# Turning a finished group's hidden state by a DMA of its 16-bit planes in place of TensorE's transposes

## What is computed

```python
h = jnp.maximum(_layernorm(x, axis=-1), 0.0)
x = x + _L3_gnn_ref(h, adj, nodemask, weight, w_ih, w_hh, b_ih, b_hh)

# _L3_gnn_ref, with A = (adj != 0)
for l in range(5):
    m = jnp.einsum('bnd,de->bne', h, weight[l])
    agg = jnp.einsum('bij,bid->bjd', A, m)
    h = _gru_cell(agg, h, w_ih, w_hh, b_ih, b_hh)   # r, z, n gates; h = (1-z)*n + z*h
return h * mask[..., None]
```

## Time and profile before

| | |
|---|---|
| device time, median of 3 runs | 686.35 us (685.84 to 688.16) |
| the profiled execution | 686.79 us, span from first to last instruction 684.7 us |
| granted PE clock, mean over the span | 0.995 |
| busy PE / DVE / ACT / POOL | 652.9 / 594.9 / 526.3 / 410.2 us |
| DMA queue q1, share of 16 engines | 23.9% |

### The profile page before, as it was taken

One profiled execution on the slowest core, in us unless ns is written; L12 is line 12 of the kernel. 1 busy time (PEld: TensorE's weight loads), 2 busy tenths in 40 slices (PEclk: granted clock), 3 DMA queues, 4 the chain that ended last, 5 costly groups with the idle time before them and its releaser, 6 DMA issues. The chain is left out here.

```text
span 684.7 us, 13204 instructions
## 1 busy us (share of the span) xinstructions
PE 652.9 (95%) x4380; PEld 424.8 (62%) x4380; DVE 594.9 (87%) x1349; ACT 526.3 (77%) x964; POOL 410.2 (60%) x367
## 2 busy tenths in 40 slices
PE   4899999999999999989999999999999999999995
PEld 3678888888888888865555444545555555555452
DVE  3877787777778877888999899999999999999995
ACT  3688888888888888867687787777877777877774
POOL 4556676677666666464774755555555555555554
PEclk9999999999999999999999999999999999999997
DMA  6111111111000110012232333333333343333532
GB/s 159 32 33 32 32 32 32 32 32 34 22 19 24 32 32 17 10 24 47 51 59 49 59 63 74 67 78 70 69 62 65 76 79 77 61 64 78 78 74 66
DMA packets 114691, 35.82 MB, mean 52 GB/s; under 512 B 87681, under 2 KB 114625, under 8 KB 114625
## 3 DMA queue, kind: packets, MB, share of 16 engines
q1 hardware_dynamic: 113424, 34.79, 23.9%
q10 hardware_dynamic: 1200, 0.20, 0.2%
HBM read 9.80 MB, written 4.19 MB: 20 GB/s over the span
## 5 line engine op out<-in xcount | busy, mean ns | idle before, releaser
L1553 POOL TENSOR_TENSOR h0T<-r,zh 128x512 f32<-128x512 f32 x80 | 104.1, 1302 | 140.4 <-DVE r L1587 140.2
L52 PE MATMUL psum<-t_parts,gru_w 128*128 128x512 f16 x720 | 181.7, 379 | 6.2 <-DVE t_parts L1577 6.2
L52 PE MATMUL psum<-h_parts,gru_w 128*128 128x512 f16 x720 | 181.8, 379 | 2.1 <-DVE r L1591 1.2
L52 PEld LDWEIGHTS psum<-h_parts,gru_w 128*128 128x128 f16 x720 | 69.7, 98 | 83.6 <-DVE r L1591 5.3
L52 PEld LDWEIGHTS psum<-t_parts,gru_w 128*128 128x128 f16 x720 | 65.4, 98 | 77.0 <-DVE t_parts L1577 15.5
L1547 POOL TENSOR_TENSOR zh<-z,h0T 128x512 f32<-128x512 f32 x80 | 102.7, 1284 | 15.0 <-ACT z L1525 14.7
L1522 ACT CAST t_parts<-psum 128x512 f16<-128x512 f32 x80 | 46.8, 585 | 60.9 <-PE psum L52 60.6
L1435 DVE CAST h_parts<-h0T 128x512 f16<-128x512 f32 x80 | 84.0, 1050 | 2.0 <-POOL h0T L1553 1.9
L691 POOL TENSOR_TENSOR prob<-prob,row_max 128x512 f32<-128x512 f32 x64 | 68.7, 1086 | 22.3 <-DVE row_max L1179 21.5
L1530 ACT ACTIVATE r<-r,gates_b 128x512 f32<-128x512 f32 x80 | 64.9, 812 | 17.5 <-DVE r L1581 17.2
L1525 ACT ACTIVATE z<-psum,gates_b 128x512 f32<-128x512 f32 x80 | 62.3, 778 | 5.8 <-PE psum L52 0.9
(11 more groups left out here) (135 smaller groups left out, 1199.4 us busy)
## 6 DMA issues: line engine op xcount, KB each, us to landing
x_all<-in_x SPq DMA_DIRECT2D x16, 256.0 KB, 3.3
adj<-in_adj SPq DMA_DIRECT2D x16, 256.0 KB, 2.9
out_x<-y SPq DMA_DIRECT2D x14, 256.0 KB, 2.3
h_nodes<-h_parts SPq DMA_TRANSPOSE x80, 3.0
out_x<-zT SPq DMA_DIRECT2D x2, 256.0 KB, 2.3
gw<-in_L_gnn_weight SPq DMA_DIRECT2D x1, 320.0 KB, 6.5
W<-in_L_gnn_W SPq DMA_DIRECT2D x2, 128.0 KB, 2.6
wi<-in_L_gnn_w_ih SPq DMA_DIRECT2D x1, 192.0 KB, 7.4
```

What stands on the lines that cost most here:

```text
L52: return nc.tensor.matmul(out, lhsT, rhs, start=start, stop=stop)
L1553: pool.tensor_tensor(state(now), by_graph(r[now.s][:, :]), by_graph(zh[now.s][:, :]), ALU.add)\
```

## The change

Twelve of the sixteen groups (those put out inside the rounds) are turned in another way; the last four stay as they were. The 32-bit numbers of a finished h are taken as two planes of 16-bit numbers. ACT copies each plane of the group into the buffer `halves` (`take_half`, two copies, in the slots e-5 and e-4, where e is the multiple of four at which the old slot list had begun the group's output and the old output came in slot e+1). SP issues one transposing DMA of all planes into `halves_nodes` in slot e-3 (`turn_halves`). ACT joins the planes into `last_h` (`put_half`, two copies, in slots e-2 and e+1). DVE makes the multiply-adds from `last_h`, two in slot e+2 and two in slot e+3, ahead of L1591 in place of after it, and SP stores in slot e+3. The new buffers are tiles of the first layers that are free by then.

```diff
+    halves, halves_nodes, last_h = first.y[3], first.adjT1[0], first.adjT
...
+    def halves_of(x):
+        return x.bitcast(U16).rearrange("p g (n t) -> p t g n", t=2)
+
+    def ended_before(j, back):
+        p, i = (j - back) // SLOTS, (j - back) % SLOTS // STREAMS
+        if (j - back) % STREAMS == 0 and 0 < p < ROUNDS and i > 0:
+            return Ended(p, i, 0)
...
-                    one_slot(p, i, s, Ended(p, i, 0) if p > 0 and i > 0 and s == 1 else None)
+                    one_slot(p, i, s)
...
+        def take_half(group, half):                                  # ScalarE
+            act.wait_ge(h_ready, group.h_count)
+            if group.count > 1:
+                act.wait_ge(halves_landed, 16 * (group.count - 1))
+            h = t["h0T"][:, bass.ds(group.first, GROUP), :]
+            a.copy(halves[:, 2 * half:2 * half + 2, :].bitcast(U16).rearrange("p u (v n) -> p (u v) n", v=2),
+                   halves_of(h)[:, half, :, :]).then_inc(halves_ready, 1)
+
+        def put_half(group, half):
+            act.wait_ge(halves_landed, 16 * group.count)
+            if group.count > 2:
+                act.wait_ge(out_ready, group.count - 2)
+            a.copy(halves_of(last_h[group.count % 2][:, :, :])[:, half, :, :],
+                   halves_nodes[:, 2 * half:2 * half + 2, :].bitcast(U16).rearrange("p u (v c) -> p (u v) c", v=2))\
+                .then_inc(last_h_ready, 1)
...
             remaining(j)                                             # between L1530 and L1535
+            for half in range(2):
+                if ended_before(j, half - 5):
+                    take_half(ended_before(j, half - 5), half)
+                if ended_before(j, 3 * half - 2):
+                    put_half(ended_before(j, 3 * half - 2), half)
...
-        def finish(group):
-            dve.wait_ge(back_psum, group.count)
+        def finish(group, first_graph):                              # VectorE
+            if group.count > GROUPS - STREAMS:
+                dve.wait_ge(back_psum, group.count - (GROUPS - STREAMS))
+                turned = P[:, BACK, :].rearrange("p (g c) -> p g c", g=GROUP)
+            else:
+                dve.wait_ge(last_h_ready, 2 * group.count)
+                turned = last_h[group.count % 2]
...
-            for g in range(GROUP):
-                last = v.scalar_tensor_tensor(out[group.buffer][:, g, :], P[:, BACK, g * 128:(g + 1) * 128],
+            for g in range(first_graph, first_graph + 2):
+                last = v.scalar_tensor_tensor(out[group.buffer][:, g, :], turned[:, g, :],
...
+            for first_graph in (0, 2):                               # between L1587 and L1591
+                if ended_before(j, 2 + first_graph // 2):
+                    finish(ended_before(j, 2 + first_graph // 2), first_graph)
...
+        def turn_halves(group):                                      # SyncE
+            sp.wait_ge(halves_ready, 2 * group.count)
+            if group.count > 1:
+                sp.wait_ge(last_h_ready, 2 * (group.count - 1))
+            sp.dma_start_transpose(halves_nodes[:, :, :].bitcast(U16).rearrange("p u (v c) -> p (u v) c", v=2),
+                                   halves[:, :, :].bitcast(U16).rearrange("p u n -> p (u n)")).then_inc(halves_landed, 16)
...
             if at(0):
                 turn(at(0))
+            if ended_before(j, -3):
+                turn_halves(ended_before(j, -3))
             if ended is not None:
                 store(ended)
+            if ended_before(j, 3):
+                store(ended_before(j, 3))
```

## The result

The changed kernel takes 683.22 us (median of 11 runs, 681.35 to 684.56) against 686.16 of the kernel before (11 runs): ratio 0.9950, 95% interval 0.9938 to 0.9962. That is 2.9 us less, with 2.6 to 4.3 us by the interval. The prediction was 683.3.

A forecast was written before the change was run, and what follows sets the result against it. PE and the DVE-POOL loop were both taken as bounds, about 4.35 us a slot. A group at 0.50 in place of 0.755 saves 12 x 0.255 = 3.1 us from the median 686.35: 683.3, range 680.5 to 709.

The forecast's parts named there:

- What bounds the kernel: Recurrent stage: PE (4.33 us a slot) and the DVE-POOL loop (4.35) both bound; at most 9.1 us to win.
- The transposes: PE: removing them from twelve groups takes away 0.44 us each, 5.3 us, all on PE's path.
- The new cost of a group: A group's four slots: finishing a group costs 0.50 us over undisturbed slots in place of 0.755.
- L1635's delay less the slacks: DVE's instruction after the pair (old L1591) comes 0.515 us late, less 0.19 of slack: 0.33 a group.
- The slacks on the way from DVE to PE and back to POOL: About 0.1 us before PE waits for L1591, and 0.09 from PE through the sigmoid L1525 to POOL.
- The copies: ACT: four copies per group at 0.6 us each fit in 0.71 us of idle time per slot; cost 0.
- SP's queue: Extra transposing DMA makes the next h_parts transpose about 0.7 us late, covered by 1.0 us; cost 0.
- My sign of a wrong SP step: PE waiting for h_nodes would show that the extra DMA's cost of 0 was wrong.
- Rival A: POOL is in before the pair's second multiply-add, which is shut out: +1.65 us a group, 706 us; chance 0.33.
- The other reading: DVE's multiply-add asks for the port after its scalar read, at 0.92 us against POOL's 0.895; spoke for POOL in first.
- Rival B: The slacks of 0.1 and 0.09 are absent, or the copy costs 0.8: 0.69 a group, 685.6 us; chance 0.14.
- rival C: Extra transpose lands after 4.8 us, first put_half holds ACT about 1.0 us in nine groups: 692 us; chance 0.05.

The follow-up runs named there:

- the best version: Changed kernel with one multiply-add in each of slots e+2 to e+5 (last of the twelve groups keeps pairs) and two buffers for the landed planes: 678.05 us.
- the last experiment: Kernel before, PE's transposes kept, multiply-adds in pairs in slots e+2 and e+3, reading PSUM, between L1588 and the cast: 681.26 us.
- without the port: Changed kernel with the pairs' first input read from a PSUM bank in place of the SBUF buffer: 680.98 us.
- the late pair: Changed kernel with one tiny DVE copy from PSUM ahead of each pair, moving the pair about 0.08 us back: 704.02 us.
- three and one: Changed kernel with three multiply-adds in slot e+2 and one in e+3: 695.97 us.
- the faster version: Changed kernel with one multiply-add in each of slots e+2 to e+5, last of the twelve groups keeping pairs, one buffer for landed planes: 681.59 us.
- the pair of 2.35 us: Changed kernel with the pairs behind L1635 in place of ahead of it, still reading SBUF: 705.75 us.

## Why the prediction was right

What bounds the kernel: right. Two loops of 4.35 us, and 9.1 us as the most that a perfect output could win; the best version won 8.2.

The transposes: the part on PE said that 0.44 us goes "all on PE's path". Left out alone they gave 0 (686.09), since the wait for L1577 took their place; where the multiply-adds were out of the way they cost 0.37 (the last experiment). The sum did not suffer, because it was made by the difference of two group costs, 0.755 and 0.50, and not by adding up what was removed; but as a sentence on the part it was wrong.

The new cost of a group: 0.50 predicted, 0.45 measured over sixteen slots. The path was the one forecast: POOL held in e+2, then L1635's delay in e+3 through PE back to POOL, which outlasts POOL's second hold and shows as 0.12 in the slot behind it. Its terms, one by one: POOL held 0.18, measured 0.16 to 0.18; L1635's delay less the slacks 0.33, measured 0.27 without the port. The slacks on the way from DVE to PE and back to POOL, 0.19 together, were thus 0.25, a little more than I read.

The copies: cost 0, right (683.09 without them). I took 0.6 for each; reading every second number lasts 0.60 and puts L1570 back by 0.51, writing every second number lasts 0.75 and puts it back by 0.62. That left ACT 0.15 or nothing of its 0.71, and DVE did not wait.

SP's queue: cost 0, nearly right for this kernel, and mis-sized. I had the next transpose 0.7 late under 1.0 of cover. It was due at 513.38 and went out at 514.46:

```profile
513.11 1.23 SPq L1664 DMA_TRANSPOSE adjT<-y  x1
...
514.46 4.75 SPq L1651 DMA_TRANSPOSE h_nodes<-h_parts  x2
```

That is 1.08 late: the copy that the extra DMA waits for lasts 0.75 in place of 0.6, and the queue leaves 0.08 us ahead of that DMA and 0.12 behind it. It stays hidden because the pairs make PE late as well: when they were thinned out, it cost 3.5 us (681.59 against 678.05). It was not hidden everywhere. My sign of a wrong SP step, PE waiting for h_nodes, is there once in the changed kernel:

```profile
459.48 2.02 SPq L1664 DMA_TRANSPOSE adjT<-y  x1
461.63 3.98 SPq L1651 DMA_TRANSPOSE h_nodes<-h_parts  x2
...
464.81 0.61 PE L53 MATMUL psum<-edges,h_nodes 128*128 128x128 f16 x8 [0.41 <-DMA h_nodes<-h_parts]
```

The extra DMA took 2.02 us to issue in place of 1.23, and that slot is 5.04; another is 4.66 in place of 4.51. Together this is 0.7 us of this execution. The kernel before has such a wait as well, 0.40 us at 647, with no extra DMA, so one case does not tell how much of it is the change's.

Rival A, which had a third of the chance, had the right price: predicted 706, and 704.02 once the pair was moved by 0.07, with POOL 0.82 later in each of two slots where I had 0.84. What decided against it is the order of the start times, 0.03 ahead or 0.04 behind. The reading of who goes first was right, but a gap of 0.03 us is near the limit of what rows of another kernel can foretell, so that the outcome fell on this side of it was in part luck. That 683.22 lies 0.1 from the forecast is luck too: a group was 0.05 cheaper than the sum, which is 0.6 us over the twelve. The other reading, that the instruction asks for the port only after its per-partition scalar is read, would have made the changed kernel lose too; it did not. The Trainium skill's rule (SBUF — State Buffer, section Who interferes with whom) that whoever issues first shuts the other out for the whole instruction agrees with all three runs, the pair, the late pair, and three and one.

Rival B (685.6) fell with the slacks, rival C (692) with landings of the extra DMA of 3.1 to 3.9 us and put_half never seen to wait.

## What to carry to other kernels

Do not price a removed instruction by its length: ask what the next instruction behind it would wait for then. Here 5.3 us of transposes came free behind the 1.03 us of multiply-adds a group on another engine, and would have cost most of their length with these out of the way. Two causes of the same delay have to be tried one by one and together.

An engine that looks full can have room at one place of its order: a cast that only waits for POOL is such a place, and so is the short time between the instruction that releases POOL and POOL's start. Move work there in pieces no larger than the room, and look at which of two instructions starts first, in hundredths of a microsecond.

When a wait is cut, read again the steps that were priced at nothing because of it; SP's late transpose appeared only in the faster version.

## What the runs showed of the hardware

A DVE instruction with both inputs in SBUF and a POOL instruction excluded each other in every row looked at here, and the order of start decided down to 0.03 us one way (DVE in, POOL held 0.16 to 0.18) and 0.04 us the other (POOL undisturbed at 1.29, DVE held 1.06). One that waits goes ahead of the other engine's next instruction, even if that is queued back to back (POOL ahead of the third multiply-add, which took 1.39 us; POOL's second instruction and DVE's second in the pair of 2.35 us). The same DVE instruction with one input in PSUM cost 0.26 us beside POOL and delayed nobody.

An ACT copy of 128x512 numbers of 16 bits lasts 0.60 us when it reads every second one and 0.75 when it writes every second one; to the next start it is 0.51 and 0.62.
